# A window-attention and Fourier kernel: the second layer cut into quarters of the width, sixteen channels apart

## The reference

```
# layer 0: shifted windows of 4x4 points, 4 heads of 16
a = window_attention(x)                       # qkv, cosine scores, bias, softmax, projection
x = x + layernorm(a)
x = x + layernorm(gelu(x @ fc1) @ fc2)
# layer 1: along the axis of 256 rows (T), for each image, column n and channel c
trend = moving_average(x, 25)
xf    = rfft(x - trend)[:, :128]
ys    = einsum('bmnc,cmk->bknc', xf, w_real + 1j*w_imag)     # a 128x128 matrix per channel
out   = trend + irfft(ys, n=256)
```

## Time and profile before

| | us |
|---|---|
| median of 3 runs | 8726.0 |
| the three runs | 8725.6, 8726.0, 8736.03 |
| the profiled execution, its own time | 8730.04 |
| its span in the profile | 8728.2 |

### The profile page before, as it was taken

One profiled execution on the slowest core, in us unless ns is written; L12 is line 12 of the kernel. 1 busy time (PEld: TensorE's weight loads), 2 busy tenths in 40 slices (PEclk: granted clock), 3 DMA queues, 4 the chain that ended last, 5 costly groups with the idle time before them and its releaser, 6 DMA issues.

```text
span 8728.2 us, 660309 instructions
## 1 busy us (share of the span) xinstructions
PE 8045.9 (92%) x293684; PEld 5316.4 (61%) x293684; DVE 5884.0 (67%) x8029; ACT 6123.9 (70%) x8530; POOL 5384.8 (62%) x5127
## 2 busy tenths in 40 slices
PE   8889999999999999999999999999999999778686
PEld 5556666666666666666666666666666665566565
DVE  1467777777777777777777777777777777222121
ACT  1468888888888888888888888888888888322121
POOL 0367777777777777777777777777777777000000
PEclk9889999999999999999999999999999999889888
DMA  3122222222222222222222222222222222799999
GB/s 99 51 48 58 57 57 57 58 57 57 56 58 58 57 57 57 57 55 55 57 58 58 57 57 57 58 57 57 56 58 58 57 56 55 239 316 323 331 316 334
DMA packets 1187112, 834.31 MB, mean 96 GB/s; under 512 B 633233, under 2 KB 1043217, under 8 KB 1182867
## 3 DMA queue, kind: packets, MB, share of 16 engines
q1 hardware_dynamic: 1182404, 698.61, 31.1%
q10 hardware_dynamic: 4608, 134.22, 3.6%
HBM read 412.97 MB, written 285.21 MB: 80 GB/s over the span
## 4 chain that ended last, share of the span: by engine, by line
PE 91%; issue 4%; DMA 4%; SPq 0%; ACT 0%; DVE 0%; ACTq 0%; POOL 0%; POOLq 0%; DVEq 0%
PE ps L501 15%; PE ps L479 14%; PE ps L542 12%; PE ps L554 11%; PE ps L462 10%; PE ps L581 10%; PE ps L526 6%; PE ps L513 6%; PE ps L450 3%; DMA out<-arena 3%; PE ps L424 1%; PE ps L415 1%; PE ps L416 1%; SPq L278 0%; ACTq L733 0%
## 5 line engine op out<-in xcount | busy, mean ns | idle before, releaser
L953 POOL TENSOR_TENSOR arena<-arena 128x512 f32<-128x512 f32 x1024 | 1044.9, 1042 | 896.8 <-PE ps L501 896.8
L479 PEld LDWEIGHTS ps<-arena 32*32 32x32 f32 x131072 | 1226.2, 106 | 509.9 <-issue 505.4
L501 PEld LDWEIGHTS ps<-arena 32*32 32x32 f32 x131072 | 1296.7, 103 | 287.5 <-issue 260.4
L501 PE MATMUL ps<-arena 32*32 32x16 f32 x131072 | 1426.2, 186 | 21.9 <-issue 20.5
L479 PE MATMUL ps<-arena 32*32 32x16 f32 x131072 | 1332.1, 180 | 25.4 <-issue 16.6
L985 POOL TENSOR_TENSOR arena<-arena 128x512 f32<-128x512 f32 x512 | 714.4, 1395 | 871.6 <-DVE arena L844 871.6
L805 DVE TENSOR_TENSOR arena<-ps,arena 128x768 f32<-128x768 f32 x1024 | 980.7, 958 | 365.6 <-PE ps L462 365.3
L542 PE MATMUL ps<-arena 64*128 64x512 f32 x4096 | 1033.2, 621 | 209.2 <-issue 206.7
L581 PE MATMUL ps<-xch,amat 128*128 128x256 f32 x4096 | 924.9, 389 | 287.2 <-ACT arena L718 196.2
L462 PEld LDWEIGHTS ps<-arena 64*128 64x128 f32 x8192 | 648.9, 188 | 837.0 <-issue 829.9
L694 ACT ACTIVATE arena<-ps,arena 128x1024 f32<-128x1024 f32 x1024 | 1131.9, 1106 | 6.7 <-PE ps L542 6.7
(11 more groups left out here) (89 smaller groups left out, 14246.7 us busy)
## 6 DMA issues: line engine op xcount, KB each, us to landing
arena<-in_x SPq DMA_DIRECT2D x4096, 32.0 KB
arena<-arena SPq DMA_DIRECT2D x1024, 128.0 KB
y<-ystripe SPq DMA_DIRECT2D x256, 512.0 KB
amat<-mix SPq DMA_DIRECT2D x512, 256.0 KB, 3.3
xch<-y SPq DMA_DIRECT2D x512, 256.0 KB, 4.0
out<-arena ACTq DMA_DIRECT2D x32, 4096.0 KB, 27.1
mix<-amat SPq DMA_DIRECT2D x64, 256.0 KB, 2.0
wri<-in_w_real SPq DMA_DIRECT2D x64, 64.0 KB, 1.8
```

The source lines that it names most:

```text
L479: ins = mm(S(sl)[r, c0 + e:c0 + 32:2], qT[r, sl, q, e:64:2], kT[r, sl, q, e:32:2], start=True, stop=True, tile_position=(32 * cg, 32 * cg))
L501: ins = mm(PV[32 * h:32 * h + 32, b, c0:c0 + N], vexp[r, sl, h, :, :], pT[r, sl, h // 2, h % 2, :], start=True, stop=True, tile_position=( ...
L953: tt(vexp.rearrange("p s h e d -> p (s h) e d")[:, :, e, :], qkv[ring(g, 4)][:, 2].rearrange("p s (h d) -> p (s h) d", h=HEADS), par[:, e: ...
```

## The change

The second layer is cut across the width. The 256 columns fall into four quarters of 64, and the quarters run one after another through the images: in phase p (35 phases in all) 16 channels are worked on, c = 16 (p mod 4) and the next 15, and quarter j takes part if 0 <= p - j < 32, with image (p - j) // 4. So quarter j begins an image one phase after quarter j - 1, each phase multiplies the 16 matrices with the columns of up to four quarters (in phases 3 to 31 all four), and in each phase from the fourth on one quarter of an image comes to its end.

- **Layout of y.** Image, row, quarter, channel, column of the quarter. `store_y` has four DMAs in place of two, of 1024 descriptors each; a descriptor is 64 columns, 256 bytes.
- **Loads.** Matrices come four channels at a time (a block: one DMA of 1 MB, pieces of 4 KB, since `mix` now keeps two channels side by side), with two buffers. Points come for eight channels at a time, one DMA of 512 KB for each active quarter (pieces of 2 KB), with two buffers. SP issues block n of the matrices when TensorE is done with block n - 2, and, behind every second block, the points of the eight channels after it. Blocks 0 and 1 of the matrices are issued before the wait for `y`.
- **TensorE.** As before 4 calls per channel, on the columns of the active quarters; eight PSUM banks in place of four. 560 channel steps in place of 512.
- **ScalarE and VectorE.** A channel's result goes to `orow` for the quarters that go on with their image. The quarter that has just begun a new image goes to `stage` (on the memory of the stripes), by an instruction of its own; with the split around that quarter a channel takes two or three instructions in place of one.
- **Stores.** At the start of each phase from 4 on, when all 16 channels of the phase before are copied out, ScalarE issues the store of the finished quarter: two DMAs of 2 MB, pieces of 16 KB. It waits first that the store of the phase before has landed, and VectorE waits for that too.
- **GpSimd.** `flush` copies `stage` (2048 values per partition) into `orow` once the store has landed; ScalarE and VectorE wait for the flush two phases later.
- **No loops.** The second layer is written out on every engine. Four buffers of the opening are two, and its memory is shared with the new rings.

```diff
-    yr = y.rearrange("b h c w -> (b h) c w")
+    y = y.rearrange("b h c w -> (b h c w)").rearrange("(b h q c n) -> b h q c n", b=B, h=H, q=4, c=C)
+    yr = y.rearrange("b h q c n -> (b h) q c n")
+    mix = mix.rearrange("c p n -> (c p n)").rearrange("(a p c n) -> a p c n", a=C // 2, p=P, c=2)
...
+        def active(p):
+            js = [j for j in range(4) if 0 <= p - j < 4 * BL1]
+            return js[0], js[-1] + 1
+
+        def staged(p):
+            return p % 4 if p >= 4 and p - p % 4 < 4 * BL1 else None
...
                 for a in range(2):
-                    sp.dma_start(
-                        yr[bass.ds(s * ROWS, ROWS), :, a * HALF:(a + 1) * HALF].rearrange("r c n -> c r n"),
-                        ystripe[ring(h, 8) // GPS][a * C:(a + 1) * C].rearrange("p r q n -> p r (q n)")).then_inc(y_out[ring(h, 8) // GPS], 16)
+                    for qq in range(2):
+                        sp.dma_start(
+                            yr[bass.ds(s * ROWS, ROWS), 2 * a + qq].rearrange("r c n -> c r n"),
+                            ystripe[ring(h, 8) // GPS][a * C:(a + 1) * C, :, 2 * qq:2 * qq + 2].rearrange("p r q n -> p r (q n)"))\
+                            .then_inc(y_out[ring(h, 8) // GPS], 16)
...
+            for n in range(2):
+                load_mats(n)
+            for i in range(2):
+                sp.wait_ge(y_out[i], 32 * NS)
+            for m in range(2):
+                load_rows(m)
+            for n in range(2, 4 * PHASES):
+                sp.wait_ge(o_ps, 4 * (n - 2) + 4)
+                load_mats(n)
+                if n % 2 == 1 and n // 2 + 1 < 2 * PHASES:
+                    load_rows(n // 2 + 1)
...
+                for k in range(2):
+                    for r in range(2):
+                        ins = mm(ps[:, x % 8, k * T + lo * 64:k * T + hi * 64],
+                                 amats[n % 2][:, jc, r * T + k * P:r * T + (k + 1) * P],
+                                 xchs[m % 2][:, lo:hi, r, jr * 64:jr * 64 + 64], start=(r == 0), stop=(r == 1))
...
+            for p in range(PHASES):
+                if p >= 5:
+                    act.wait_ge(rows_out, 32 * (p - 4))
+                if p >= 4:
+                    rows(p)
+                if staged(p - 2) is not None:
+                    act.wait_ge(flushed, flushes(p - 2))
+                for x in range(16 * p, 16 * p + 16, 2):
+                    put(x)
```

More of the change, by code:

```diff
@@ L268, in swin_then_fourier, with rows_count, flushes @@
         consts_in = 16 * 41
+        def active(p):
[3 more added lines that the diff above has]
+            return p % 4 if p >= 4 and p - p % 4 < 4 * BL1 else None
+        def rows_count(m):
+            spans = [active(v // 2) for v in range(m % 2, m + 1, 2)]
+            return 16 * sum(hi - lo for lo, hi in spans)
+        def flushes(p):
+            return sum(1 for m in range(p + 1) if staged(m) is not None)
         block = ctx.enter_context(nc.Block())
@@ L364, in _, with load_mats, load_rows @@
                     store_y((i - 12) // GPS, Group(i - 12, GPS - 1))
[L365 to L366 removed]
             for j in range(2):
                 sp.wait_ge(m_out[j], 16 * (NCH // 2))
[L371 to L384, removed]
+            def load_mats(n):
+                b = n % BLOCKS
+                sp.dma_start(amats[n % 2].rearrange("p (a c) n -> p a (c n)", a=2),
+                             mix[2 * b:2 * b + 2].rearrange("a p c n -> p a (c n)")).then_inc(mats_in[n % 2], 16)
+            def load_rows(m):
+                p = m // 2
+                lo, hi = active(p)
+                for j in range(lo, hi):
+                    c = m % 8 * 8
+                    src = y[(p - j) // 4, :, j, c:c + 8, :].rearrange("(r t) c n -> t r (c n)", r=2)
+                    sp.dma_start(xchs[m % 2][:, j], src).then_inc(rows_in[m % 2], 16)
+            for n in range(2):
[9 more added lines that the diff above has]
+                    load_rows(n // 2 + 1)
         @block.tensor
@@ L572, in _, with channel @@
             over_groups(pe, step, 1)
[L575 to L578, removed]
+            def channel(x):
+                n, jc, m, jr = x // 4, x % 4, x // 8, x % 8
+                lo, hi = active(n // 4)
+                if jc == 0:
+                    pe.wait_ge(mats_in[n % 2], 16 * (n // 2 + 1))
+                if jr == 0:
+                    pe.wait_ge(rows_in[m % 2], rows_count(m))
+                if x >= 8:
+                    pe.wait_ge(o_dve if x % 2 else o_act, (x - 8) // 2 + 1)
                 for k in range(2):
                     for r in range(2):
-                        ins = mm(ps[:, j, k * T:(k + 1) * T], amat[j][:, r * T + k * P:r * T + (k + 1) * P],
-                                 xch[j][:, r * T:(r + 1) * T], start=(r == 0), stop=(r == 1))
+                        ins = mm(ps[:, x % 8, k * T + lo * 64:k * T + hi * 64],
+                                 amats[n % 2][:, jc, r * T + k * P:r * T + (k + 1) * P],
+                                 xchs[m % 2][:, lo:hi, r, jr * 64:jr * 64 + 64], start=(r == 0), stop=(r == 1))
                 ins.then_inc(o_ps, 1)
[L585 to L590, removed]
+            for x in range(16 * PHASES):
+                channel(x)
         @block.scalar
@@ L736, in _, with put @@
-            act.wait_ge(rows_out, 64 * BL1)
+            def put(x):
+                p, c = x // 16, x % 64
+                lo, hi = active(p)
+                st = staged(p)
+                src = ps[:, x % 8, :].rearrange("p (k n) -> p k n", k=2)
+                act.wait_ge(o_ps, x + 1)
+                ins = None
+                runs = [(lo, hi)] if st is None else [(lo, st), (st + 1, hi)]
+                for a, b in runs:
+                    if a < b:
+                        ins = f(orow[:, :, a * 64:b * 64, c], src[:, :, a * 64:b * 64], ACT.Copy)
+                if st is not None:
+                    ins = f(stage[p % 2][:, x % 16], src[:, :, st * 64:st * 64 + 64], ACT.Copy)
+                ins.then_inc(o_act, 1)
@@ L1022, in _, with flush @@
             over_groups(pool, step, 8)
+            def flush(p):
+                j, c = p % 4, p % 4 * 16
+                pool.wait_ge(o_act, 8 * p + 8)
+                pool.wait_ge(o_dve, 8 * p + 8)
+                pool.wait_ge(rows_out, 32 * (p - 3))
+                pool.tensor_copy(orow[:, :, j * 64:j * 64 + 64, c:c + 16],
+                                 stage[p % 2].rearrange("p c k n -> p k n c")).then_inc(flushed, 1)
+            for p in range(PHASES):
+                if staged(p) is not None:
+                    flush(p)
 def arrays_of(inputs):
```

100 lines of the change are left out of this document (57 added, 43 removed).

## The result

| | us |
|---|---|
| before, median | 8725.8 |
| after, median of 4 runs | 9083.4 (9061.8 to 9097.5) |
| ratio | 1.0405, 95% interval 1.0393 to 1.0418 |
| after, the profiled execution and its span | 9061.8 and 9060.0 |

The change makes the kernel 4% slower. The forecast was 8820, 94 us longer; it became 358 us. The sign was right, the size was not. The profiled execution after, the fastest of its four, is 331.8 us longer than the one before, where the sum said 93.

A forecast was written before the change was run, and what follows sets the result against it. TensorE was taken to bound the first layer; in the second it stood still 44 us per image around the store. Terms of +29 (second layer) and +64 (first) gave 8820 against a median of 8726.0; range 8610 to 9350.

The forecast's parts named there:

- A: First layer: small descriptors each cost their own time, a wait of about 5 us behind each store, total 9345; chance 0.23.
- B (real sharing): Second layer: loads get half or more of the DMA engines beside the store, phase 32 us, total 8640; chance 0.20.
- D: Second layer: the stall of 8.3 us per phase leaves the store nearly as exposed as before; held within the forecast.
- C: Both layers: the clock doesn't fall and the load of x keeps its place, total 8694; chance 0.15.
- The price of 18 ns: First layer: cost of a 256-byte descriptor, taken from the load of x at 225 GB/s; +0.2 us per store.
- So 0.5 us for each of 128 stores, +64 us: First layer: four stores ahead of the load of x delay it, 0.2 us for descriptors and 0.3 for issues.
- The phase is 36.1 us ... 38.1: Second layer: a full phase with TensorE waiting 8.3 us, 36.1 us; with 2.0 for the fallen clock, 38.1.
- The rate of 400 GB/s: Second layer: assumed DMA rate for loads in pieces of 2 and 4 KB, 21.0 us of loads per phase.
- my 1272: Second layer: the sum of start, all phases and last store in us, against 1242.9 before, so +29.

The follow-up runs named there:

- old_y: The changed kernel with y in its old layout: two stores of 512-byte descriptors per stripe, points read in pieces of 256 bytes; 8990.5 us, ratio 1.0295.
- four_stores_512: The kernel before, its store of a stripe cut by rows into four DMAs in place of two, same 512-byte descriptors; 8802.0 us, ratio 1.0081.
- late_store: The changed kernel with the store of a stripe moved on SP behind the next load of x; 8855.2 us, ratio 1.0141 to the kernel before.

## Why the prediction was right and wrong

**The mechanisms held, two terms of the sum did not.** A wait once per phase behind the second block, of nearly the length of the store, with a drop of the clock behind it; and a first layer made slower by the four stores ahead of the load of x. Of the rivals, A fell: 256 bytes into HBM took 19 ns, not 35. The Trainium skill, "DMA: Bandwidth & Descriptors", Specifications, has a read-modify-write below 512 bytes; no price of it shows in this trace, in which 256 bytes took about half of the 35 ns of 512. B (real sharing) fell by the queue's counts; D came close to what happened: the wait of 10.5 us is as long as the whole store of 9.8. C fell: the clock did drop, in both layers, and the load of x came later.

The price of 18 ns was right by luck in part. The prediction held that bytes from 64 partitions set one rate at three sizes, but the load of x, its row for 256 bytes, goes to 128 partitions. There, too, 256 bytes take 18 ns: so they also do in `old_y`, where the points are read in such pieces to 128 partitions (the median of its pieces). No run tells for 256 bytes whether the 64 partitions or the descriptor sets the price.

**Two terms were too small; some 218 of the 239 us missing in the profiled executions (331.8 - 93) are in these steps.**

*"So 0.5 us for each of 128 stores, +64 us".* It measured +204, 1.6 us a store. The price of a descriptor was right and the delay was not. The step that failed is that the issue of two more DMAs lies mostly inside the time in which SP is blocked, 0.3 us: `four_stores_512` measured that alone at 0.6 us of delay and 71 us in all. With twice the descriptors the delay was 1.2 us, so these brought another 0.6 where the sum had 0.2; why SP is blocked for so long is not shown. And I left out what a late load does to the clock. In the group that began its turning at 831.07 us, behind a wait of 1.13 us, the clock fell for the stretch 833 to 837, and the group took 15.56 us:

```profile
833.00:837.00 4.00, 4.00 (x20) 1.48 (x16) 2.38 (x5) 1.62 (x4) 1.39 (x1) 0.57 0.23 52
831.07:846.63 15.56, 15.08 (x564) 9.07 (x565) 9.94 (x15) 10.40 (x15) 9.35 (x10) 0.89 0.15 34
```

From 600 to 7300 us the clock record has 109 us at the lower level, 7 in the kernel before (two stretches, with no wait of the matmuls for x). It comes in 28 stretches, each in a group that began behind a wait, and these groups took 1.67 us longer than the 90 behind a wait without a fall: 47 of the 204 us. With the waits gone (`late_store`) there is none. Waits of 0.96 to 1.22 us came before the 28 falls, but 44 waits of the same length passed without one; what decides is open.

*"The phase is 36.1 us ... 38.1".* It measured 40.9. The wait ends 24.4 us behind the end of the last phase (8251.7 to 8276.05), where I had 22.2. The rate of 400 GB/s held only in its later part: DMA moved 265 GB/s in the 6.0 us from 8252.7, in which the first pieces of matrices and of points are slow to come (some 0.75 us for a piece of 4 KB at first, 0.16 later), and 420 GB/s, store and loads together, from 8258.7 to the end of the wait. And the restart cost 2.8 us, not 2.0: the first block took 9.8 us (8235.15 to the next block's issue at 8244.92) instead of 7.0. The two make 28 x 2.8 = 78 of the 96 us that the second layer, counted from the landing of `y`, is above my 1272. Most of the rest is in the ramp: phases 0 to 2 took 74.7 us (7700.34 to 7775.08), not 63, as their short blocks of 3.8 to 5.4 us don't cover a load of 1 MB (waits of 7.4 us in all, the 3.49 above the longest) and the first 33 us ran at the lower clock (0.50 and 0.53), behind the wait of 20.47. And the start took 8.7 us instead of 4: the 2 MB of matrices issued ahead of the wait for `y` stood in the queue ahead of the first points.

**The range** (8610 to 9350) held the time by its width: 9083 lies between the forecast's 8760 to 8880 and A's 9100 to 9420, nearer to A, whose mechanism was not at work, so that the range held is luck. The chance of slower, 0.60, was on the right side. The forecast's own range was much too narrow: both terms rested on assumptions of tenths of a us (0.3, 0.5, 1.4) that are multiplied by 128 or 28.

## What to carry to other kernels

Look at what a queue carries behind the instruction that a change makes longer: the same four stores cost 207 us in the trace (228 between the medians) more ahead of a load that is just in time than behind it. When a large store and the loads of the next work run beside each other on two queues, compare the sizes of their pieces, for the DMA engines here gave each queue one piece in turn; cut or spread the store so that what lies ahead of a load is less than what the buffers cover. A wait that repeats a hundred times must be known to a tenth of a us, or its term is a range and not a number.

## What the runs showed of the hardware

- Turns of one piece each between two hardware queues: 201 to 203 pieces in 8 us, at 16 KB and 2 KB, and 408 to 408 in 4 us, at 2 KB both.
- Waits of 0.56 to 1.22 us of TensorE were followed by a stretch at the lower clock in 28 of 118 cases; the one of some 10.5 us by a restart at the lower clock in each of the 28 phases with a store.
- Transfers from 64 partitions ran at 214 to 231 GB/s of a full share, whether in pieces of 256 bytes, 512 bytes or 2 KB; into HBM 256 bytes took 19 ns, with no extra price for being short beside 35 ns for 512. Pieces of 256 bytes to 128 partitions ran at the same rate (the load of x, 225 GB/s).
- An engine that issues a DMA of many descriptors stands longer in the issue: 13.40 us of ScalarE for four DMAs of 1024 pieces of 1 KB, 8 us for four of 512 pieces, 2.5 us for four of 256, 1.11 us for two of 128 pieces of 16 KB.
